# Fewer filler matmuls and an earlier attention projection in the first layer of a two-layer transformer kernel

## The reference

```python
# x: (8, 512, 128)
xn = layernorm(x)
x = x + attention0(xn) + ffn0(xn)      # softmax(q k / sqrt(8)) v, 16 heads, then out_w, out_b
                                       # ffn0: block_quant -> w_fc -> gelu -> block_quant -> w_proj
xn = layernorm(x)
x = x + attention1(xn) + experts(xn)   # sum over 8 experts of (silu(x Wg) * (x Wu)) Wd
```

## Time and profile before

| what | before |
|---|---|
| median of 3 runs | 1461.66 us (1459.96 to 1463.94) |
| the profiled execution | 1459.96 us |
| its span | 1458.2 us |
| busy: PE, VectorE, ScalarE, GpSimd | 90%, 70%, 57%, 50% |

### The profile page before, as it was taken

The page is one execution under the profiler, slowest core; times in us unless marked ns, Lnnn a source line. Parts: engine busy times, 40 slices in busy tenths (PEclk is TensorE's granted clock), DMA queues, the critical chain, the costliest instruction groups (busy, mean ns, idle before and its releaser), DMA issues. The chain is left out here.

```text
span 1458.2 us, 23453 instructions
## 1 busy us (share of the span) xinstructions
PE 1309.7 (90%) x8264; PEld 765.8 (53%) x8264; DVE 1017.8 (70%) x2380; ACT 825.3 (57%) x1236; POOL 733.3 (50%) x853
## 2 busy tenths in 40 slices
PE   3888988989889953999999999999999999999978
PEld 1444444444444422566665666566565665656645
DVE  4566676766767512788787877878787787877843
ACT  1455666666666621565665656656566566656640
POOL 5243464655644544455554655645556555545530
PEclk7799999999999975899999999999999999999997
DMA  5222232423423224110011100100100100000013
GB/s 170 67 79 75 89 110 87 149 86 102 121 77 109 83 67 115 34 48 29 21 48 31 49 30 21 47 31 27 52 27 20 52 27 30 27 31 9 16 38 102
DMA packets 54258, 88.64 MB, mean 61 GB/s; under 512 B 9943, under 2 KB 20700, under 8 KB 54142
## 3 DMA queue, kind: packets, MB, share of 16 engines
q1 hardware_dynamic: 52990, 86.61, 19.0%
q10 hardware_dynamic: 1152, 0.52, 0.2%
HBM read 41.69 MB, written 44.31 MB: 59 GB/s over the span
## 5 line engine op out<-in xcount | busy, mean ns | idle before, releaser
L1143 POOL TENSOR_TENSOR a_h_lo<-a_h,a_h_hi 128x512 fp32r<-128x512 f32 x256 | 328.8, 1284 | 164.1 <-ACT a_h_hi L1190 163.0
L650 DVE TENSOR_REDUCE l_mx<-bank_pair 128x2 f32<-128x1024 f32 (+3 forms) x256 | 203.1, 819 | 129.0 <-PE bank_pair L890 128.2
L1252 DVE SCALAR_TENSOR_TENSOR a_h<-a_h,bank_pair 128x512 f32<-128x512 f32 x256 | 175.4, 685 | 138.9 <-ACT a_h L1186 138.9
L131 PE MATMUL bank_pair<-st 24*128 24x512 f32 (+3 forms) x1024 | 206.1, 388 | 62.2 <-ACT l_E L736 26.7
L166 DVE CUSTOM_DVE_ANT_0 bank_pair<-bank_pair,mask 128x512 f32<-128x512 f32 (+3 forms) x512 | 238.1, 517 | 6.5 <-PE bank_pair L131 6.4
L1190 ACT ACTIVATE a_h_hi<-a_h 128x512 fp32r<-128x512 f32 x256 | 161.6, 631 | 132.2 <-DVE a_h L1258 128.9
L1197 ACT ACTIVATE a_E<-bank_pair 128x1024 f32<-128x1024 f32 (+1 forms) x192 | 169.6, 883 | 115.0 <-PE bank_pair L138 115.0
L736 ACT ACTIVATE l_E<-bank_pair 128x1024 f32<-128x1024 f32 (+1 forms) x192 | 168.4, 879 | 85.6 <-PE bank_pair L138 85.5
L131 PEld LDWEIGHTS bank_pair<-st 24*128 24x128 f32 x1024 | 104.7, 187 | 204.2 <-issue 164.3
L190 POOL TENSOR_SCALAR_AFFINE_SELECT a_E<-a_E 128x256 f32<-128x256 f32 (+1 forms) x192 | 94.7, 493 | 216.1 <-ACT a_E L1197 216.0
L1258 DVE TENSOR_TENSOR a_h<-a_h,bank 128x512 f32<-128x512 f32 x256 | 176.0, 688 | 31.3 <-DVE a_h L1252 6.0
(11 more groups left out here) (133 smaller groups left out, 2199.3 us busy)
## 6 DMA issues: line engine op xcount, KB each, us to landing
st<-stack_d SPq DMA_DIRECT2D x256, 96.0 KB
stack_d<-l_q_k_hi SPq DMA_DIRECT2D x64, 256.0 KB, 3.0
stack_d<-l_q_k_lo SPq DMA_DIRECT2D x32, 256.0 KB, 3.3
o_d<-l_O SPq DMA_DIRECT2D x32, 256.0 KB, 2.1
o_d<-a_O SPq DMA_DIRECT2D x32, 256.0 KB, 2.0
l_at<-o_d SPq DMA_DIRECT2D x8, 256.0 KB, 3.4
l_share<-rden_d SPq DMA_DIRECT2D x8, 256.0 KB, 3.2
a_wst<-wg_in SPq DMA_DIRECT2D x8, 256.0 KB, 2.8
```

The source lines that it names most:

```text
L131: return nc.tensor.matmul(bank[:, col:col + w], st[rows, 0, bass.ts(t, P)], st[rows, 1, 0:w], start=first, stop=last)
L650: ins = nc.vector.tensor_reduce(out, pair[:, :, col:col + width(kb)], AX.X, ALU.max)
L1143: nc.gpsimd.tensor_tensor(h_lo[:, q % RH, :], h[:, q % RH, :], h_hi[:, q % RH, :].bitcast(F32), ALU.subtract).then_inc(h_lo_ready, 1)
L1252: nc.vector.scalar_tensor_tensor(hq, hq, 1.0, g_bank[:, :], ALU.add, ALU.mult).then_inc(silu_ready, 1)
```

## The change

Two things change, both in `layer0`. The table of fillers goes: `fill(g, 4)` is no longer called, and `fill(g, 1)` to `fill(g, 3)` issue two matmuls each, but five for n = 1 in u = 1. And the attention projection of u = 3 moves ahead of unit 4, on PE and in the list that assigns banks; VectorE adds its result before the maxima of unit 5.

```diff
-FILLERS = ((2, 2, 2, 2), (10, 2, 2, 0), (2, 2, 4, 3), (2, 2, 2, 3))
@@ units_in_order
         scores_and_keys(3)
+        put(("A", 1, b - 1), u == 3 and 0 <= b - 1 < B)
         scores_and_keys(4)
-        put(("A", 1, b - 1), u == 3 and 0 <= b - 1 < B)
         scores_and_keys(5)
@@ layer0, VectorE
                 if S:
                     maxima_of(g + 1, 4)
-                if S:
-                    maxima_of(g + 1, 5)
                 if u == 3 and ok(y1):
                     add_attention(y1)
                 if S:
+                    maxima_of(g + 1, 5)
                     negations(g + 1)
@@ layer0, TensorE, fill
-                    keep_warm(nc, pv_bank, identr, FILLERS[g % QUADS_A_BATCH][n - 1])
+                    keep_warm(nc, pv_bank, identr, 5 if g % QUADS_A_BATCH == 1 and n == 1 else 2)
@@ layer0, TensorE, the loop over steps
                 scores_and_keys(g, 3)
                 if u == 2 and ok(b + 1):
                     turn_x(b + 1)
-                fill(g, 4)
+                if u == 3 and ok(y1):
+                    project_attention(y1)
                 scores_and_keys(g, 4)
                 if in_range(g - 1):
                     PV(g - 1, 0)
                     PV(g - 1, 1)
-                if u == 3 and ok(y1):
-                    project_attention(y1)
```

## The result

| | before | changed |
|---|---|---|
| median | 1461.68 us (1459.96 to 1463.94, 4 runs) | 1506.48 us (1501.61 to 1509.05, 4 runs) |
| profiled execution, its span | 1459.96, 1458.2 us | 1510.67, 1509.0 us |

What follows compares the result with a forecast made beforehand. PE, the busiest engine, was taken to bound layer 0, in a bank-pair loop with ACT and DVE. Fillers -0.7, clock falls +19 and the wait +5 made +23 us on 1459.96: 1483, forecast as 1485 us; range 1465 to 1499.

Steps and rivals of the forecast that it cites:

- The direction: Whole kernel: the change makes it slower, chance 0.88.
- the fillers off the path: Layer 0, PE: leaving out 120 of 336 fillers gives almost nothing back directly, 0.1 us a time, 0.7 us in all.
- the holes of 1.35, 0.7, 1.6 and 1.8 us: PE idle times: u = 2 at n = 3 and n = 4, u = 1 early, u = 3 before the moved projection.
- the wait's 0.7 us a step: u = 3: the moved projection waits for POOL's atT, so the step ends 0.7 us later; seven times, 5 us.
- The number of added falls: Layer 0, batches 1 to 7: PE's clock drops to half 2.3 more times per group, 16 more in all.
- the chances of the prediction: Falls per thinned stretch: 8 or 9 of 10 in u = 2 and u = 3, 6 early u = 1, 2 u = 0.
- the price of a fall: Layer 0 steps: each added fall of the clock costs 1.2 us on average, bounds 0 and 1.56; 16 cost 19 us.
- the part absorbed early in u = 1: u = 1: the late, half-empty stretch absorbs a part of what a fall behind the early stretch costs; no separate size.
- Rival 1: Layer 0: the clock falls no more often, only the projection's new wait counts, +5 us, 1467 us; chance 0.14.
- Rival 2: u = 3: atT arrives in time, the projection replaces fillers for nothing; faster, 1446, with few falls about 1454 us; chance 0.05.
- Rival 3: Layer 0: the clock falls more often but mostly inside holes, 0.3 us each; 1471 us with the wait's +5; chance 0.16.

Runs made afterwards that it cites:

- the first experiment: The kernel before with only the thinner fillers of the change, the attention projection left behind unit 4: 1496.23 us, ratio 1.022.

## Why the prediction was wrong

- The direction, the fillers off the path, the holes of 1.35, 0.7, 1.6 and 1.8 us, and the wait's 0.7 us a step were right, each within 0.1 us.
- The number of added falls was right, 16 forecast, and in good part by luck. Between 99 us and the end of the last step the changed kernel has 21, the kernel before 6 (the prediction took five, all late in u = 1; one is early in u = 1 and one in u = 2). By the chances of the prediction the added ones were to be 6 in u = 2, 6 in u = 3, 3 in u = 1 and 1 in u = 0; they are 2, 6, 2 and 5. The busy time ahead, by which the stretches were sorted, did not find them: 1.09 us busy kept the clock in u = 2.
- The step that failed is the price of a fall: "The bounds are 0 and 1.56; I take 1.2 as a mean". The upper bound came from the single kind of fall that the trace of before has in its steady part, one of 3.4 us. The 21 falls of the changed kernel last 119 us together, 5.7 us each; nine are of 6.8 or 10.2 us. Of the 44.0 us to the end of the last step 3.2 are there already at the step that ends at 93.8 us (90.6 before), and the wait is 6 x 0.74 = 4.4. The other 36.4 us over 15 more falls are 2.4 each. With 2.4 for 1.2 the sum is 16 x 2.4 + 5 - 0.7 = 43 us; measured were 44.8. For a fall of 3.4 us the price was nearly right, and the part absorbed early in u = 1 too: such falls 6 to 7 us into a step u = 1 cost 0.7 to 0.9 us.
- Longer falls were to be had from the trace of before: it has falls of 7, 10 and 24 us, where PE is thin at the end of layer 0 (mean clock 0.59 from 519 to 580 us). I read the price from the steady part alone. Those falls stand where PE has little to do, and give no price of their own.
- Rival 1 fell with the first experiment: its 34.5 us come without the moved projection. Its trace has 19 falls between 99 us and the last step's end, and no pause of PE there is longer than 2.02 us. The rule of the Trainium skill (TensorE: Matmul & The Clock Gate, section "HAM oscillation") that a long unbroken pause is what lowers the clock does not account for these falls. Rival 2 fell twice: atT was late, and with atT early the bank is. Rival 3 is shown wrong by the steps of all traces here: without the projection's wait a fall of 3.4 us alone in a step costs 0.7 to 2.2 us, mostly 1.4 to 1.7, never 0.3, and one of 10.2 us 3.0 to 3.7 us.
- I counted busy time and nothing else. The fillers work on 128 rows, and what stands behind the early hole of u = 1 are mostly scores on 24; the fillers on 32 rows point to rows as what was left out of the count, and do not prove it. Why one fall lasts 3.4 us, the next 10.2 and one 30.7 is open.

## What to carry to other kernels

A filler matmul that costs nothing on the path can be worth more than the code around it: judge it by what the clock does without it, and look first for the hole behind which the trace shows falls, for three more fillers there gave 5 us here. Keep fillers on all rows, since on a quarter of them 62 us were lost here; a quarter of the weights' columns was enough. A price read from one event bounds only events of that kind; when a change makes a stretch thinner than any in the trace, its upper bound has to be taken from the longest events of the whole trace, and even those, 24 us in the kernel before, were exceeded once, by one of 30.7. Before work is moved up into a hole, list everything that it waits for, its output bank's readers too.

## What the runs showed of the hardware

A fall of the clock is a whole event: u = 3 steps were 0.0 or 1.6 us longer where only that place was thinned, nothing between. Falls in the steady part lasted 3.4, 6.8 or 10.2 us, and one 30.7 us. At half clock a PE that was busy in all of 12 us did not get the full clock back for 10, and one busy in 28.79 of 30.7 us did not for the 30.7. A stretch of 3.2 us with 1.09 us busy kept the clock, and one with 2.80 us busy was followed by a fall. With fillers on 32 instead of 128 rows the kernel was 62 us slower, with 32 instead of 128 columns of weights the same.
